# Attention probabilities transposed head by head (77 keys) instead of in 128-wide blocks, in a gated cross-attention and feed-forward kernel

## The chip, the cores and the metric

One NeuronCore of one Trainium2 chip runs the whole program. The time is device microseconds of one execution. The engines are named as in the profile: PE is TensorE's matmuls and PEld its weight loads, DVE is VectorE, ACT is ScalarE, POOL is GpSimd, SP is SyncE (here only a DMA queue).

## The reference, cut to what matters

Batch 16, 512 queries of width 512, 77 context tokens a batch, 16 heads of 32. All is float32.

```python
q = layernorm(x) @ Wq.T + bq              # (16, 512, 512)
k = ctx @ Wk.T + bk;  v = ctx @ Wv.T + bv # (16, 77, 512)
scores = einsum('bhnd,bhmd->bhnm', q, k) / sqrt(32)   # 16 heads, 512 x 77
attn = softmax(scores, axis=-1)
o = einsum('bhnm,bhmd->bhnd', attn, v)    # the values product
x = x + tanh(g_xattn) * (o @ Wo.T + bo)
x = x + tanh(g_ffn) * ffn(layernorm(x))   # 512 -> 2048 -> 512, with sines and relu
```

## The kernel before, in words

Three blocks follow each other: `setup` (weights turned and split, keys and values of all batches computed and kept in DRAM), `attention`, and `ffn`. The change touches the attention, and in the setup how the values are cleared, stored and loaded.

Projections, scores and output products run in three passes of split operands (`matmul3`, L56: high by high, high by low, low by high, type fp32r). The transposes of the probabilities and the values products take plain float32.

The attention handles a batch in four slots, one for each group `g` of four heads. A slot multiplies the queries of its four heads with a block-diagonal matrix of keys (`k_diag`, four times 77 = 308 columns) into two score banks, each of two tiles of 128 queries. DVE takes the peaks (L1063), ACT the exponentials with their sums (L1017), DVE the reciprocals (L1068), and POOL multiplies them into `probs` (L855). Two groups make a *pair* (eight heads, 616 columns of probabilities for each query); there are 32 pairs. `probs` has the 128 queries of a tile on the partitions and the 616 keys of a pair in a row, padded with zeros to 640.

The values product needs the keys on the partitions. So PE transposes `probs` (L900): the pair's 640 columns are five blocks `c` of 128 keys, and one block takes four transposes, one for each tile of queries, into one of two PSUM banks `t_bank`. The block is copied into `probsT` by DVE (`copy_probs`, L1059, blocks 0 to 2) or ACT (`copy_late_probs`, L1002, blocks 3 and 4), and the bank may be written again. In a transpose the data is what is loaded as weights, and the 128x128 identity is what is streamed; the profile writes this as 128*128 128x128 (weights, then streamed).

Blocks of 128 keys don't end where heads of 77 end. So a head's keys lie in one or two blocks, and `v_diag` holds its values at the same rows, with zeros elsewhere in the block (cleared once in setup, filled for each batch by twelve small DMAs, `load_values`). A head's product (L948) is one or two matmuls of 128 rows x 32 columns of weights with 512 queries streamed, added up in PSUM: six for each group of four heads, twelve a pair. The four heads of a group write four different strips of 32 partitions of one bank `m_bank`. In the profile each of these float32 matmuls is two instructions.

The order on PE is written out by hand, slot by slot (L966 to L988). In an even slot (`g` 0 or 2): scores, queries of the next slot, transposes of block 2 of the pair before, an output product of an earlier batch. In an odd slot (`g` 1 or 3): transposes of blocks 3 and 4, scores, queries of the next slot, output product, transposes of blocks 0 and 1 of the next pair, then the values products of the pair. Every engine runs its list in order and waits on counting semaphores: a transpose waits for the copy that last read its bank, a query projection for the subtraction that read its `m_bank` (`m_split`), the scores of a slot for their queries (`queries_lo`, L1078, on DVE).

The order on DVE in an even slot is peaks, `heads_lo` (L1085), peaks, copies of blocks 0 and 1, reciprocal, half of the rows of a layer norm or of a turn (L205, L214), copy of block 2, `queries_lo`, the other half of the rows, `gate_output` (L1091), reciprocal. In an odd slot it is peaks, peaks, `x_lo` (L1073) or the sums of a layer norm (L180), reciprocal, `queries_lo`, `gate_output`, reciprocal, `heads_lo`. ACT in an odd slot copies blocks 3 and 4, then exponentials, `queries_hi`, exponentials, `heads_hi` (L1029) twice.

Of the kernel before, what the change touches and what calls it, by code (L numbers as in the profile page):

```python
# [30 lines left out]
F32 = mybir.dt.float32  # L31
# [51 lines left out]
def gated_attention_ffn_kernel(nc, x, ctx_in, g_xattn, g_ffn, wq, bq, wk, bk, wv, bv, wo, bo,  # L83
# [13 lines left out]
    PC = -(-2 * GC // P)  # L97
    NC = -(-GC // P)
    FROM = (0, GC - (NC - 1) * P)
# [12 lines left out]
    assert N == 512 and D == 512 and G == KT == NT == 4 and B % CB == 0 and NC == 3 and PC == 5 and FT == 16  # L112
# [12 lines left out]
    with ExitStack() as whole:  # L125
# [130 lines left out]
        v_diag = [sb(att, f"v_diag{i}", [P, 2, NC, HG, 2 * DH]) for i in range(2)]  # L256
# [10 lines left out]
        pieces = [[], []]  # L267
        for second in range(2):
            for j in range(HG):
                r = FROM[second] + j * M  # L270
                end = r + M
                while r < end:
                    n = min(end, (r // P + 1) * P) - r
                    pieces[second].append((j, r // P, r % P, M - (end - r), n))
                    r += n
        assert len(pieces[0]) == len(pieces[1])
        PIECES = len(pieces[0])

        strips = []
        for j in range(HG):  # L280
            strip = []
            for second in range(2):
                of_head = [c for h, c, _, _, _ in pieces[second] if h == j]
                strip += [(second, c, i == 0, i == len(of_head) - 1) for i, c in enumerate(of_head)]
            strips.append(strip)
        assert all(len(strip) == len(strips[0]) for strip in strips)
        ends = [max((step, j) for j in range(HG) for step, piece in enumerate(strips[j]) if piece[0] == second)
                for second in range(2)]

# [8 lines left out]
        def load_values(queue, b, loaded):  # L298

            for second in range(2):  # L300
# [5 lines left out]
        def by_head(row):  # L306

            return row.rearrange("p (g h d) -> p g h d", g=G // 2, d=DH)

        def by_place(row):  # L310

            return row.rearrange("p (h g d) -> p g h d", g=G // 2, d=DH)

        def setup():
            with ExitStack() as st:  # L315
# [116 lines left out]
                def _(pool):  # L432
# [6 lines left out]
                    pool.memset(k_diag[:, :, :, :].bitcast(F32), 0.0)  # L439
# [4 lines left out]
                    pool.wait_ge(cleared, 2)  # L444
# [154 lines left out]
                def _(dve):  # L599
# [20 lines left out]
                    def values_sum(r, j):  # L620
                        n = v_rows(j)
                        dve.wait_ge(v_full, RT * r + j + 1)
                        if not (isinstance(r, int) and r == 0):
                            dve.wait_ge(v_stored[j], 16 * r)
                        dve.tensor_tensor(by_place(v_sum[j][0:n, :]), by_head(v_bank[j % 2][0:n, :]), by_head(bv_rows[0:n, :]),
                                          ALU.add)\
                           .then_inc(v_summed, 1)
# [86 lines left out]
        def attention(st):  # L714
# [4 lines left out]
            probs = [sb(st, f"probs{i}", [P, NT, PC * P]) for i in range(G // 2)]  # L719
            probsT = sb(st, "probsT", [P, PC, N])  # L720
# [22 lines left out]
            EARLY_C, LATE_C = range(NC), range(NC, PC)  # L743
# [34 lines left out]
            def transposed(pair, c):  # L778
                n = PC * pair + c + 1
                return n, (n - 1) % 2  # L780
# [71 lines left out]
            def _(pool):  # L852
# [14 lines left out]
                for i in range(G // 2):  # L867
                    pool.memset(probs[i][:, :, 2 * GC:PC * P], 0.0)
# [20 lines left out]
            def _(pe):  # L889
                def transpose_probs(pair, c):  # L890
                    n, bank = transposed(pair, c)
                    if c in (0, NC - 1):

                        pe.wait_ge(probs_ready, 4 * pair + (4 if c else 2))
                    if c >= 2:
                        pe.wait_ge(t_copied, NC * pair + c - 1)
                    elif pair:
                        pe.wait_ge(late_copied, 2 * (pair - 1) + c + 1)
                    for tile in range(NT):
                        tr = pe.transpose(t_bank[bank][:, tile * P:(tile + 1) * P],  # L900
                                          probs[pair % 2][:, tile, c * P:(c + 1) * P], ident[:, :])
# [29 lines left out]
                def value_products(pair, values):  # L931


                    pe.wait_ge(late_copied, 2 * (pair + 1))
                    b = pair // 2
                    if b == 0:
                        pe.wait_ge(first_values_loaded, 16 * PIECES * 2)
                    else:
                        pe.wait_ge(values_loaded[b % 2], 16 * PIECES * 2 * ((b + 1) // 2))
                    pe.wait_ge(m_split, values[0][0] - 2)  # L940
# [569 lines left out]
```

## Time and profile before

| | |
|---|---|
| median of 3 runs | 2146.89 us (2144.68 to 2148.01) |
| the profiled execution | 2147.3 us, its span 2145.5 us |
| PE busy | 2114.2 us (99%), 10321 matmuls |
| PEld busy | 1710.1 us (80%) |
| DVE busy | 1433.8 us (67%) |
| ACT busy | 1164.1 us (54%) |
| POOL busy | 398.6 us (19%) |
| granted TensorE clock, mean | 0.997 |

The span is the time from the first to the last instruction; the execution's own time lies 1.8 us above it. A line of a timeline gives the start of a run of like instructions, the time until the last of them ended, and their count. Matmuls overlap, so the mean duration of one is longer than the distance to the next. A row of one line's or one tile's instructions gives the least, median and largest duration of one in ns. A row of waits says who was waited for: total us, how often, the longest.

### The profile page before, as it was taken

The page shows a single profiled execution, that of the slowest core. Times are in us where ns is not written, and L with a number is a line of the kernel's source. Part 1 is how long each engine was busy: PE and PEld are TensorE (multiplying, and loading weights), DVE is VectorE, ACT ScalarE, POOL GpSimd, SP SyncE. Part 2 cuts the span into 40 slices and gives each one's busy share as a digit, 9 for nine tenths or more (in the row PEclk, how much of TensorE's full clock was granted, in tenths as well). Part 3 has the DMA queues.
Part 4 walks back from the last instruction along what each step waited for, and adds up shares of the span by engine and source line. Part 5 has one row for each costly group of instructions (what it writes and reads, how often), then busy time and mean ns, then how long its engine had stood idle before and what let it go on. Part 6 is the DMA issues. An engine that isn't in the chain of part 4 may idle for free.

```text
span 2145.5 us, 29054 instructions
## 1 busy us (share of the span) xinstructions
PE 2114.2 (99%) x10321; PEld 1710.1 (80%) x10321; DVE 1433.8 (67%) x2457; ACT 1164.1 (54%) x3463; POOL 398.6 (19%) x324
## 2 busy tenths in 40 slices
PE   8889999999999999999999999999999999999999
PEld 7767777777777678888888888888888888888887
DVE  4587877787777477666665666656666566566654
ACT  3387877777777455444445444444454444444443
POOL 3044444433443310010110101101101011010110
PEclk9999999999999999999999999999999999999999
DMA  7464445455544352231212312213123121231210
GB/s 217 128 144 110 121 126 120 121 119 117 128 113 101 118 146 75 59 77 50 51 59 59 79 59 41 77 41 79 59 59 79 53 46 62 57 79 59 40 40 20
DMA packets 372475, 181.88 MB, mean 85 GB/s; under 512 B 294374, under 2 KB 308938, under 8 KB 372330
## 3 DMA queue, kind: packets, MB, share of 16 engines
q1 hardware_dynamic: 371258, 179.52, 33.0%
q8 instruction: 81, 1.33, 0.3%
q0 software_dynamic: 640, 0.47, 0.1%
q14 instruction: 64, 0.52, 0.1%
q10 hardware_dynamic: 432, 0.04, 0.0%
HBM read 106.34 MB, written 56.85 MB: 76 GB/s over the span
## 4 chain that ended last, share of the span: by engine, by line
PE 63%; DVE 1%; ACT 0%; issue 0%; ACTq 0%; DVEq 0%
PE pair_bank L56 32%; PE m_bank L56 32%; DVE w_split L1402 0%; DVE hidden L1436 0%; DVE turns L1432 0%; DVE sine L1429 0%; ACT relu L1362 0%; ACT hidden L1371 0%; ACT turns L1373 0%; DVE stats L180 0%; DVE relu L1419 0%; DVE x_in L205 0%; ACT sine L1378 0%; DVE residual L1444 0%; DVE mean L190 0%
## 5 line engine op out<-in xcount | busy, mean ns | idle before, releaser
L56 PE MATMUL pair_bank<-w_split,relu 128*128 128x512 f32 x3072 | 738.4, 389 | 3.9 <-DVE relu L1419 3.2
L56 PE MATMUL m_bank<-xT,w_split 128*128 128x512 f32 x3024 | 726.4, 389 | 0.0
L56 PEld LDWEIGHTS pair_bank<-w_split,relu 128*128 128x128 f32 x3072 | 576.2, 188 | 125.4 <-issue 3.7
L56 PEld LDWEIGHTS m_bank<-xT,w_split 128*128 128x128 f32 x3024 | 567.5, 188 | 117.9
L1378 ACT ACTIVATE sine<-turns 128x512 f32<-128x512 f32 x256 | 161.8, 632 | 393.3 <-DVE turns L1432 393.3
L1017 ACT ACTIVATE exps<-pair_bank,lowest 128x77 f32<-128x77 f32 x1024 | 317.6, 352 | 59.8 <-DVE lowest L1063 59.7
L1362 ACT ACTIVATE relu<-hidden 128x512 fp32r<-128x512 f32 x256 | 161.9, 632 | 330.9 <-PE m_bank L56 231.6
L1419 DVE SCALAR_TENSOR_TENSOR relu<-hidden,relu 128x512 fp32r<-128x512 f32 x256 | 181.3, 708 | 201.7 <-ACT relu L1362 201.7
L1436 DVE SCALAR_TENSOR_TENSOR hidden<-sine,sine_gain,hidden 128x512 f32<-128x512 f32 x256 | 197.2, 770 | 169.9 <-ACT sine L1378 169.9
L200 POOL TENSOR_TENSOR rstd<-var_eps,minus_half 128x4 f32<-128x4 f32 x32 | 38.3, 1196 | 1198.3 <-DVE var_eps L196 1198.3
L1017 ACT ACTIVATION_READ_ACCUMULATOR exps<-pair_bank,lowest 128x1 f32 x1024 | 238.9, 234 | 0.0
L855 POOL TENSOR_TENSOR probs<-exps,exp_inv 128x616 f32<-128x616 f32 x128 | 158.6, 1239 | 300.1 <-DVE exp_inv L1068 300.1
L1432 DVE TENSOR_TENSOR turns<-turns,sine 128x512 f32<-128x512 f32 x256 | 192.2, 751 | 8.8
L56 PE MATMUL m_bank<-xT,wqT 128*128 128x512 f32 x768 | 188.1, 394 | 0.0
L1429 DVE TENSOR_SCALAR sine<-turns 128x512 f32<-128x512 f32 x256 | 122.2, 477 | 93.1 <-ACT turns L1373 92.6
L56 PE MATMUL m_bank<-woT,oT 128*128 128x512 f32 x720 | 180.0, 399 | 0.6 <-DVE oT L1085 0.6
L1373 ACT ACTIVATE turns<-m_bank,turns_phase 128x512 f32<-128x512 f32 x256 | 173.9, 679 | 0.0
L1371 ACT ACTIVATE hidden<-m_bank,columns 128x512 f32<-128x512 f32 x256 | 171.9, 671 | 1.9 <-PE m_bank L56 1.9
L56 PEld LDWEIGHTS m_bank<-xT,wqT 128*128 128x128 f32 x768 | 142.9, 190 | 27.1 <-DVE xT L1073 0.2
L56 PEld LDWEIGHTS m_bank<-woT,oT 128*128 128x128 f32 x720 | 133.4, 189 | 30.3 <-DVE oT L1085 1.5
L56 PEld LDWEIGHTS pair_bank<-k_diag,qT 128*128 128x128 f32 x768 | 111.2, 191 | 37.9 <-issue 30.9
L56 PE MATMUL pair_bank<-k_diag,qT 128*128 128x308 f32 x768 | 127.8, 315 | 9.9 <-PEq L315 5.3
(127 smaller groups left out, 1723.5 us busy)
## 6 DMA issues: line engine op xcount, KB each, us to landing
residual<-in_x_dram SPq DMA_DIRECT2D x64, 256.0 KB, 2.7
x_scratch<-residual SPq DMA_DIRECT2D x64, 256.0 KB, 2.1
x_in<-x_scratch SPq DMA_DIRECT2D x16, 1024.0 KB, 5.5
residual<-x_scratch SPq DMA_DIRECT2D x64, 256.0 KB, 3.3
out_dram<-residual SPq DMA_DIRECT2D x64, 256.0 KB, 2.1
quad_scratch<-x_in SPq DMA_DIRECT2D x60, 256.0 KB, 5.1
x_in<-quad_scratch SPq DMA_DIRECT2D x60, 256.0 KB, 4.4
x_in<-in_x_dram SPq DMA_DIRECT2D x8, 1024.0 KB, 5.6
```

Of the source, the lines that this page charges most:

```text
L56: mm = pe.matmul(out, stationary(s), moving(m), start=first and n == 0, stop=last and n == len(PASSES) - 1)
L200: pool.tensor_tensor(rstd[:, :], var_eps[:, :], minus_half[:, :], ALU.pow).then_inc(rstd_ready, 1)
L855: pool.tensor_tensor(probs[g // 2][:, HALF * half:HALF * (half + 1), g % 2 * GC:(g % 2 + 1) * GC] .rearrange("p n (h m) -> p n h m", m=M), ...
L1017: e = act.activation(exps[half][:, n, h * M:(h + 1) * M], pair_bank[half][:, n, h * M:(h + 1) * M], ACT.Exp, bias=lowest[half][:, i:i + 1] ...
L1362: act.activation(relu[f % 2][0][:, :], hidden[f % 2][:, :], ACT.Relu).then_inc(relu_hi, 1)
L1371: act.activation(hidden[f % 2][:, :], m_bank[f % 2][:, :], ACT.Identity, bias=b1_col[:, f % FT:f % FT + 1])
L1373: act.activation(turns[:, :], m_bank[f % 2][:, :], ACT.Identity, scale=0.1 / TWO_PI, bias=turns_phase[:, f % FT:f % FT + 1]).then_inc(h_re ...
L1378: act.activation(sine[:, :], turns[:, :], ACT.Sin, scale=TWO_PI_BELOW).then_inc(sine_ready, 1)
L1419: dve.scalar_tensor_tensor(out=relu[f % 2][1][:, :], in0=hidden[f % 2][:, :], scalar=0.0, in1=relu[f % 2][0][:, :].bitcast(F32), op0=ALU.m ...
L1429: dve.tensor_scalar(sine[:, :], turns[:, :], ROUND_MAGIC, ROUND_MAGIC, ALU.add, ALU.subtract)\
L1432: dve.tensor_tensor(turns[:, :], turns[:, :], sine[:, :], ALU.subtract).then_inc(part_ready, 1)
L1436: dve.scalar_tensor_tensor(out=hidden[f % 2][:, :], in0=sine[:, :], scalar=sine_gain[:, f % FT:f % FT + 1], in1=hidden[f % 2][:, :], op0=A ...
```

## The change: one block for each head

The blocks of the transposes are the heads: eight of 77 keys a pair, in place of five of 128. A transpose has 77 columns of weights and the same 128 columns of identity streamed; it writes 77 partitions. A head's values product is one matmul of 77 rows, eight a pair in place of twelve. The values of a batch lie as they are, 77 rows of 512, in `v_rows_of`, loaded by one DMA; nothing is cleared. The padding of `probs` is gone.

The transposes of heads 2 and 3 take the place of those of block 2, heads 4 and 5 that of blocks 3 and 4, heads 0 and 1 that of blocks 0 and 1. Heads 6 and 7 are transposed in the odd slot, after the queries and ahead of the output product. DVE copies heads 0 to 3 in the even slot and head 7 in the odd slot behind `queries_lo`; ACT copies heads 4 and 5 at the start of the odd slot and head 6 behind `queries_hi`, ahead of the second exponentials. The two groups' products follow each other, group by group.

```diff
-        v_diag = [sb(att, f"v_diag{i}", [P, 2, NC, HG, 2 * DH]) for i in range(2)]
+        v_rows_of = [sb(att, f"v_rows_of{i}", [P, D]) for i in range(2)]
...
         def load_values(queue, b, loaded):
-            for second in range(2):
-                for j, c, p0, m0, n in pieces[second]:
-                    h = HG * second + j
-                    queue.dma_start(v_diag[b % 2][p0:p0 + n, second, c, j, :],
-                                    v_rows_all[bass.ds(M * b + m0, n), 2 * DH * h:2 * DH * (h + 1)]).then_inc(loaded, 16)
+            queue.dma_start(v_rows_of[b % 2][0:M, :], v_rows_all[bass.ds(M * b, M)]).then_inc(loaded, 16)
...
-                    for i in range(2):
-                        pool.memset(v_diag[i][:, :, :, :, :], 0.0).then_inc(cleared, 1)
...
-            probs = [sb(st, f"probs{i}", [P, NT, PC * P]) for i in range(G // 2)]
-            probsT = sb(st, "probsT", [P, PC, N])
+            probs = [sb(st, f"probs{i}", [P, NT, 2 * GC]) for i in range(G // 2)]
+            probsT = sb(st, "probsT", [P, 2 * HG, N])
...
+            DVE_HEADS, ACT_HEADS = (0, 1, 2, 3, 7), (4, 5, 6)
+            def copies_until(pair, h):
+                of_dve = h in DVE_HEADS
+                heads = DVE_HEADS if of_dve else ACT_HEADS
+                return (t_copied if of_dve else late_copied), len(heads) * pair + heads.index(h) + 1
...
-                def transpose_probs(pair, c):
-                    n, bank = transposed(pair, c)
-                    if c in (0, NC - 1):
-                        pe.wait_ge(probs_ready, 4 * pair + (4 if c else 2))
-                    if c >= 2:
-                        pe.wait_ge(t_copied, NC * pair + c - 1)
+                def transpose_probs(pair, h):
+                    n, bank = transposed(pair, h)
+                    if h in (0, HG):
+                        pe.wait_ge(probs_ready, 4 * pair + (4 if h else 2))
+                    if h >= 2:
+                        pe.wait_ge(*copies_until(pair, h - 2))
                     elif pair:
-                        pe.wait_ge(late_copied, 2 * (pair - 1) + c + 1)
+                        pe.wait_ge(*copies_until(pair - 1, h + 2 * HG - 2))
                     for tile in range(NT):
-                        tr = pe.transpose(t_bank[bank][:, tile * P:(tile + 1) * P],
-                                          probs[pair % 2][:, tile, c * P:(c + 1) * P], ident[:, :])
+                        tr = pe.transpose(t_bank[bank][0:M, tile * P:(tile + 1) * P],
+                                          probs[pair % 2][:, tile, h * M:(h + 1) * M], ident[:, :])
...
                 def value_products(pair, values):
-                    pe.wait_ge(late_copied, 2 * (pair + 1))
+                    pe.wait_ge(*copies_until(pair, DVE_HEADS[-1]))
+                    pe.wait_ge(*copies_until(pair, ACT_HEADS[-1]))
...
-                    for step in range(len(strips[0])):
-                        if step == 1:
-                            pe.wait_ge(m_split, values[1][0] - 2)
+                    for second, (n, bank, _) in enumerate(values):
+                        pe.wait_ge(m_split, n - 2)
                         for j in range(HG):
-                            second, c, first, last = strips[j][step]
-                            mm = pe.matmul(m_bank[values[second][1]][j * DH:(j + 1) * DH, :],
-                                           v_diag[b % 2][:, second, c, j, pair % 2 * DH:(pair % 2 + 1) * DH],
-                                           probsT[:, second * (NC - 1) + c, :], start=first, stop=last)
-                            if (step, j) in (ends[0], ends[1]):
-                                mm.then_inc(m_full, 1)
+                            column = (2 * (pair % 2) + second) * P + j * DH
+                            mm = pe.matmul(m_bank[bank][j * DH:(j + 1) * DH, :], v_rows_of[b % 2][0:M, column:column + DH],
+                                           probsT[0:M, second * HG + j, :], start=True, stop=True)
+                        mm.then_inc(m_full, 1)
...
                         if s.queries:
                             queries(b + (g == 3), (g + 1) % G, *s.queries[:2])
-                        if not s.odd and s.pair is not None:
-                            transpose_probs(s.pair, NC - 1)
+                        if s.pair is not None:
+                            for h in (6, 7) if s.odd else (2, 3):
+                                transpose_probs(s.pair, h)
                         if s.output:
                             block_output(*s.output)
...
                     if s.queries:
                         queries_hi((g + 1) % G, *s.queries[:2])
+                    if s.odd and s.pair is not None:
+                        copy_late_probs(s.pair, 6)
                     if s.score:
                         exponentials(2 * G * b + 2 * g + 2, 1)
...
                     if s.queries:
                         queries_lo((g + 1) % G, *s.queries[1:])
+                    if s.odd and s.pair is not None:
+                        copy_probs(s.pair, 7)
```

## Rows read from the trace of the kernel before

**Rows 1.** The page's slices: the granted TensorE clock in tenths.
```profile
PEclk9999999999999999999999999999999999999999
```

**Rows 2.** Windows: stretch, us; busy PE, PEld, DVE, ACT, POOL (count); clock, DMA.
```profile
200.00:700.00 500.00, 500.00 (x2958) 387.90 (x2956) 389.80 (x715) 373.39 (x1845) 202.00 (x165) 1.00 0.49 117
131.00:150.50 19.50, 16.84 (x107) 12.40 (x106) 18.13 (x36) 17.51 (x90) 10.43 (x9) 1.00 0.49 72
```

**Rows 3.** Waits from 200 to 700 us: total us, times, longest.
```profile
ACT oT L1029 <- PE m_bank L948: 66.5, 50, 2.4
...
DVE oT L1085 <- ACT oT L1029: 63.1, 25, 2.5
...
PEld pair_bank L56 <- DVE qT L1078: 0.5, 2, 0.2
```

**Rows 4.** Timeline of PE: start, us, instructions, in one pair.
```profile
307.01 1.03 PE L900 MATMUL t_bank<-ident,probs 128*128 128x128 f32 x8
307.97 2.78 PE L948 MATMUL m_bank<-probsT,v_diag 128*32 128x512 f32 x24
310.68 1.96 PE L56 MATMUL pair_bank<-k_diag,qT 128*128 128x308 f32 x12
...
315.25 0.60 PE L900 MATMUL t_bank<-ident,probs 128*128 128x128 f32 x4
315.61 3.04 PE L56 MATMUL m_bank<-woT,oT 128*128 128x512 f32 x12
```

**Rows 5.** Values products and transposes, 300 to 400 us: least, median, largest ns.
```profile
L948 PEld LDWEIGHTS m_bank<-probsT,v_diag x120: 106/110/110, 308.0 to 388.0; 128*32 128x32 f32 x120
L948 PE MATMUL m_bank<-probsT,v_diag x120: 592/592/617, 308.0 to 388.4; 128*32 128x512 f32 x120
...
L900 PEld LDWEIGHTS t_bank<-ident,probs x100: 138/140/142, 306.8 to 397.4; 128*128 128x128 f32 x100
L900 PE MATMUL t_bank<-ident,probs x100: 270/272/273, 307.0 to 397.5; 128*128 128x128 f32 x100
```

**Rows 6.** Timeline of PEld: loads of the third and the sixth round of these products.
```profile
308.43 0.13 PEld L948 LDWEIGHTS m_bank<-probsT,v_diag 128*32 128x32 f32 x4 [0.30 <-issue]
...
309.71 0.13 PEld L948 LDWEIGHTS m_bank<-probsT,v_diag 128*32 128x32 f32 x4 [0.30 <-issue]
```

**Rows 7.** Setup's context transposes, 36.46 to 36.50 us: 52 rows, then 128.
```profile
L476 PE MATMUL pair_bank<-ident,ctx_raw x2: 263/296/329, 36.3 to 36.4; 52*128 52x52 f32 x1, 128*128 128x128 f32 x1
```

**Rows 8.** Groups by line and shape: the block copies, and one operation on 52 partitions.
```profile
L1059 DVE COPY probsT<-t_bank 128x512 f32<-128x512 f32 x75 | 48.6, 676 | 0.4 <-PE t_bank L900 0.4
...
L1002 ACT ACTIVATE probsT<-t_bank 128x512 f32<-128x512 f32 x52 | 28.8, 621 | 6.8 <-PE t_bank L900 6.8
...
L625 DVE TENSOR_TENSOR v_sum<-pair_bank,bv_rows 128x512 f32<-128x512 f32 x8 | 5.5, 690 | 10.1 <-PE pair_bank L56 10.1
...
L625 DVE TENSOR_TENSOR v_sum<-pair_bank,bv_rows 52x512 f32<-52x512 f32 x4 | 2.7, 680 | 6.3 <-PE pair_bank L56 6.3
```

**Rows 9.** Timelines of DVE and PE where an even slot meets an odd one.
```profile
297.85 0.68 DVE L1059 COPY probsT<-t_bank 128x512 f32<-128x512 f32 x1
298.45 0.73 DVE L1078 SCALAR_TENSOR_TENSOR qT<-m_bank,columns,qT 128x512 fp32r<-128x512 f32 x1
...
300.02 0.74 DVE L1091 SCALAR_TENSOR_TENSOR residual<-m_bank,tanh_g,residual 128x512 f32<-128x512 f32 x1
...
300.84 0.80 DVE L1063 TENSOR_REDUCE lowest<-pair_bank 128x8 f32<-128x616 f32 x1
...
298.92 1.03 PE L900 MATMUL t_bank<-ident,probs 128*128 128x128 f32 x8
299.71 1.94 PE L56 MATMUL pair_bank<-k_diag,qT 128*128 128x308 f32 x12
```

**Rows 10.** Waits from 120 to 152 us, the first pairs.
```profile
PE t_bank L900 <- DVE probsT L1059: 2.0, 2, 1.6
```

**Rows 11.** The values' DMA issues on SP's queue in the attention: least, median, largest ns.
```profile
L303 SPq DMA_DIRECT2D v_diag<-v_scratch x180: 269/307/720, 121.5 to 667.7; - x180
```

More of the change, by code:

```diff
@@ L111, in gated_attention_ffn_kernel @@
     NVEC = 4 * FT + 2 * G
-    assert N == 512 and D == 512 and G == KT == NT == 4 and B % CB == 0 and NC == 3 and PC == 5 and FT == 16
+    assert N == 512 and D == 512 and G == KT == NT == 4 and B % CB == 0 and FT == 16
     x1 = nc.dram_tensor("x1_scratch", [B, N, D], F32).ap()
@@ L264, in gated_attention_ffn_kernel @@
         first_values_loaded = sem(whole, "first_values_loaded")
-        pieces = [[], []]
-        for second in range(2):
[L269 to L288, printed above, removed]
         def load_keys(queue, b, pair, loaded):
@@ L776, in attention, with transposed @@
             values_of = {s.pair: s.values for s in slots if s.values}
-            def transposed(pair, c):
-                n = PC * pair + c + 1
+            def transposed(pair, h):
+                n = 2 * HG * pair + h + 1
                 return n, (n - 1) % 2
@@ L968, in _ @@
                     if not s.score:
+                        for h in (4, 5) if s.odd else (2, 3):
+                            transpose_probs(s.pair, h)
                         block_output(*s.output)
-                        for c in LATE_C if s.odd else (NC - 1,):
-                            transpose_probs(s.pair, c)
+                        for h in (6, 7) if s.odd else ():
+                            transpose_probs(s.pair, h)
                     else:
                         if s.odd and s.pair is not None:
-                            for c in LATE_C:
-                                transpose_probs(s.pair, c)
+                            for h in (4, 5):
+                                transpose_probs(s.pair, h)
                         for half in range(2):
@@ L979, in _ @@
                             queries(b + (g == 3), (g + 1) % G, *s.queries[:2])
[L980 to L981 removed]
+                        if s.pair is not None:
+                            for h in (6, 7) if s.odd else (2, 3):
+                                transpose_probs(s.pair, h)
                         if s.output:
@@ L984, in _ @@
                         if s.next_pair is not None:
-                            for c in range(NC - 1):
-                                transpose_probs(s.next_pair, c)
+                            for h in (0, 1):
+                                transpose_probs(s.next_pair, h)
                     if s.values:
@@ L997, in _, with copy_late_probs @@
             def _(act):
-                def copy_late_probs(pair):
-                    for c in LATE_C:
-                        n, bank = transposed(pair, c)
-                        act.wait_ge(t_full, n)
-                        act.activation(probsT[:, c, :], t_bank[bank][:, :], ACT.Copy).then_inc(late_copied, 1)
+                def copy_late_probs(pair, h):
+                    n, bank = transposed(pair, h)
+                    act.wait_ge(t_full, n)
+                    act.activation(probsT[0:M, h, :], t_bank[bank][0:M, :], ACT.Copy).then_inc(late_copied, 1)
                 def x_hi(b):
@@ L1034, in _ @@
                     if s.odd and s.pair is not None:
-                        copy_late_probs(s.pair)
+                        for h in (4, 5):
+                            copy_late_probs(s.pair, h)
                     if s.score:
@@ L1053, in _, with copy_probs @@
             def _(dve):
-                def copy_probs(pair, c):
-                    n, bank = transposed(pair, c)
+                def copy_probs(pair, h):
+                    n, bank = transposed(pair, h)
                     dve.wait_ge(t_full, n)
-                    if c == 0 and pair:
+                    if h == 0 and pair:
                         dve.wait_ge(m_full, values_of[pair - 1][0][0])
-                    dve.tensor_copy(probsT[:, c, :], t_bank[bank][:, :]).then_inc(t_copied, 1)
+                    dve.tensor_copy(probsT[0:M, h, :], t_bank[bank][0:M, :]).then_inc(t_copied, 1)
                 def peaks(unit, half):
@@ L1104, in _ @@
                         if s.pair is not None:
-                            for c in range(NC - 1):
-                                copy_probs(s.pair, c)
+                            for h in (0, 1):
+                                copy_probs(s.pair, h)
                         if s.score:
@@ L1113, in _ @@
                         if s.pair is not None:
-                            copy_probs(s.pair, NC - 1)
+                            for h in (2, 3):
+                                copy_probs(s.pair, h)
                     else:
```

25 lines of the change are left out of this document (5 added, 20 removed).

## The prediction

> **What bounds the kernel now.** I read the granted clock first: full speed in every slice, so no time is lost to it [rows 1]. Then the busy times by stretch. From 200 to 700 us, 25 of the 32 pairs, PE is busy for all 500 us, DVE for 390 and ACT for 373 [rows 2]. As a busy PE may hide gaps, I then read the waits of that stretch: the scores waited twice for DVE's query subtraction, 0.5 us in all, while ACT and DVE each stood idle about 2.5 us a pair until the values products were done (66.5 us in 50 waits, of which the first of each pair is the long one; 63.1 us in 25) [rows 3]. So the steady attention is bound by the sum of PE's work, and what the change adds to or takes from that sum is the first term. Last I read PE's timeline for the distances between its instructions, since durations overlap [rows 4].
>
> **A transpose.** Eight of them take 1.03 us to the end of the last [rows 4], and one lasts 0.272 us [rows 5]: (1.03 - 0.272) / 7 = 108 ns from one to the next. The four at 315.25 give (0.60 - 0.272) / 3 = 109 ns, and the output product behind them starts on time, at 315.61. I take 0.1085 us.
>
> **A values product.** The 24 instructions of a pair start in rounds of four, one for each head. The weight loads of the third and the sixth round stand 309.71 - 308.43 = 1.28 us apart, three rounds [rows 6]: 0.427 us a round. Six rounds are 2.56 us; from the first product to the scores behind them pass 2.71 us [rows 4], so entering and leaving costs 0.15 us, which stays.
>
> **What sets the price of a transpose with 77 columns.** This decides the sign, and no such transpose is in the trace. A product of 512 streamed columns lasts 592 ns, a transpose of 128 lasts 272 [rows 5]: 320 ns for 384 columns, 0.833 ns a column. That gives 512 columns 427 ns, which is the distance between rounds, and 128 columns 107 ns, which is the distance between transposes. So both are bound by what they stream. The change leaves that as it is: 128 columns of identity for each transpose. What shrinks from 128 to 77 columns is the weight load. Is it what binds? In setup a transpose of 52 rows, then one of 128, follow a change of shape, so that their loads are uncovered: 263 and 329 ns [rows 7]. By the rate, a transpose of 52 streamed columns should last 272 - 76 x 0.833 = 209 ns; it is 54 longer, and the one of 128 is 329 - 272 = 57 longer. So a load of 128 columns costs some 55 ns when nothing hides it, half of the 107 that a transpose streams, and it is hidden in a run of them. I take 0.1085 us for the new transpose too. The lower end is a price that goes with the columns loaded, 0.1085 x 77/128 = 0.065 us. Between lies the slope of the two loads, 110 ns for 32 columns and 140 for 128 [rows 5], 0.31 ns a column: 51 columns fewer save 16 ns, 0.092 us. The upper end is a load that stays uncovered, as after the changes of shape in setup: 0.1085 + 0.055 = 0.164 us. Nothing points there, as all transposes of a run have one shape. I take the row nearest in what it does, today's transpose.
>
> The Trainium skill (TensorE: Matmul & The Clock Gate, section "LDWEIGHTS (loading the stationary operand)") gives a load as its columns divided by 1.2, in ns. As an estimate from that page, 128 columns take 107 ns and 77 take 64, which would fit the distance of 108 just as well with the load as its bound. The uncovered loads of some 55 ns [rows 7] speak against it for transposes; what it would make of the time is rival A.
>
> **PE's sum.** Twelve transposes more: 12 x 0.1085 = 1.30 us. Two rounds fewer, as eight products in place of twelve are four rounds of four heads in place of six: 2 x 0.427 = 0.85 us. Net +0.45 us a pair, and for 32 pairs +14.3 us. There is one more run of transposes a pair; entering and leaving a run costs no more than some ns (315.25 + 4 x 0.1085 = 315.68, and the output product's first matmul was already in at 315.61), so nothing.
>
> **The copies.** They cost by their row, not by partitions: 680 ns on 52 and 690 on 128 [rows 8]. So DVE gets two more copies, 2 x 0.676 = 1.35 us a pair, and ACT one more, 0.62 us. Both have 2.5 us of idle time ahead of the values products [rows 3], which covers copy 7 and copy 6, both in the odd slot. What waits behind them: on ACT the second exponentials, then POOL's probabilities of that half, which PE wants only a slot later; on DVE the gate of the output, which the second group's products wait for. PE itself gets two runs more between its queries and those products, 8 x 0.1085 = 0.87 us, so the gate comes no later against PE than before. The new waits, heads 6 and 7's copies ahead of the next pair's transposes and of the values products, have the output product (12 matmuls, some 2.8 us) between the transposes and the wait. Cost: nothing; without the cover up to 0.68 us a pair.
>
> The tight place is the even slot. There copy 3 is added ahead of `queries_lo`, which the next slot's scores wait for. In the pair at 298 us copy 2 starts at 297.85 and `queries_lo` ends at 298.45 + 0.73 = 299.18; the scores start at 299.71 [rows 9]. One copy later it ends at 299.86; the scores, behind four more transposes (0.44 us), are due at 300.15. It fits by 0.3 us, so I cost it at nothing. The peaks at 300.84 come behind a gate at 300.02 [rows 9]; both are up to 0.7 us later on DVE against 0.44 on PE, and the odd slot's idle time takes the rest up.
>
> **The first pairs.** From 131 to 150.5 us DVE is busy 18.13 of 19.5 us [rows 2], and transposes waited 2.0 us for its copies [rows 10]. There the two copies count instead of PE's net: 1.35 - 0.45 = 0.9 us more for a pair, for one pair or two. I take +1 us, the ends are 0 and 2.
>
> **Loads and clearing.** Twelve issues of some 0.307 us a batch on SP's queue become one [rows 11]. SP gets to its stores about 3.4 us sooner, but nobody on PE waited for a load in the steady stretch. POOL's clearing in setup is long done when the first values come. Nothing either way.
>
> **Sum.** 14.3 + 1 = 15.3 us on the profiled execution's own 2147.3: 2162.6. The median of the runs lies 0.4 us below that execution, so 2162 us, 0.7% slower.
>
> **Rivals.**
>
> *A. A transpose costs by the columns loaded.* For it: 108 ns would also fit a load as the bound. Against it: the rate of 0.833 ns that explains both forms, and the uncovered loads. Fully proportional: 32 x 0.065 - 20 x 0.1085 = -0.09, with the products -0.94 us a pair, -30 us: 2117. At 0.092 us it is 32 x 0.092 - 2.17 - 0.85 = -0.08 us a pair: 2144. It ends on the other side, faster, for any transpose under (2.17 + 0.85) / 32 = 94 ns.
>
> *B. DVE becomes late in the even slot.* For it: only 0.3 us of room at 299.86 against 300.15, and rows there that last longer than elsewhere. Then copy 3 delays `queries_lo` and with it the scores. If its whole 0.68 us lands on PE in the sixteen slots with a layer norm, +11 us: 2173; in all 32, +22: 2184. Against it: the scores waited for DVE twice in 25 pairs.
>
> *C. The heads' products of 77 rows don't run four at a time.* Then 16 instructions take 16 x 0.427 = 6.8 us, 4.3 more than now, +137 us: about 2300. Against it: the heads still write four different strips, and only the count of rows is new. With it goes the upper end above: 0.164 us would make 32 x (32 x 0.164 - 2.17 - 0.85) = +71 us, 2219.
>
> **How the numbers follow.** Forecast 0.73, A 0.13, B 0.12, C 0.02. The forecast's own range is 2158 to 2167. The range for 8 in 10 reaches up into B as far as 2177 and down to 2154, where a transpose costs 0.100 us; it leaves out most of A, the far end of B, and C. A measurement of this kernel tells some 0.2%, 4.3 us, from no change. Of A's 0.13, 0.10 is faster and 0.03 within 0.2%; with 0.01 for gaps that take up the forecast's cost, same is 0.04; slower is the rest, 0.86.
>
> **What would show it.** Right: transposes of 77 columns 108 ns apart, runs of eight in 1.03 us; four rounds of products, some 1.85 us from the first product to the scores; pairs 0.45 us longer; no waits of PE on DVE or ACT between 200 and 700 us. Wrong: runs of eight in 0.8 us or less (A), scores waiting for `queries_lo` (B), rounds of fewer than four (C), or a clock below full speed in a slice.

## The result and the profile after

The changed kernel takes 2169.08 us (median of 4 runs, 2168.72 to 2171.05) against 2147.28 us (2144.68 to 2148.01) for the kernel before beside it: ratio 1.0106, 95% interval 1.0088 to 1.0123, so 21.8 us slower. The forecast was 2162, the range 2154 to 2177. The direction and the main term held; two terms that I had costed at almost nothing make up the difference. The time lies above the forecast's own range of 2158 to 2167; the part of the range that it fell in was added for rival B, which, as shown below, isn't the cause. The profiled run took 2168.72 us, its span is 2166.9. Of all runs below, one execution of 5524 us with the late layer norm is left out of the times.

Cut at the first values product of the third pair, of the last but one and of the last, the two spans give the table below. The forecast in it is split by its own terms: ahead of the first cut lie three pairs' transposes and two pairs' products, 3 x 1.30 - 2 x 0.85, and the +1 for the first pairs; behind the last one pair's products.

| stretch | before, us | after, us | difference | forecast |
|---|---|---|---|---|
| to the third pair | 170.87 | 177.83 | +6.96 | +3.2 |
| 28 pairs | 546.09 | 557.50 | +11.41 | +12.6 |
| the last pair | 11.26 | 14.88 | +3.62 | +0.45 |
| behind it (rest, FFN) | 1417.26 | 1416.70 | -0.56 | -0.85 |

PE's timeline after, in the steady attention, answers to [rows 4]:

```profile
317.05 1.04 PE L862 MATMUL t_bank<-ident,probs 128*77 128x128 f32 x8
318.01 1.92 PE L905 MATMUL m_bank<-probsT,v_rows_of 77*32 77x512 f32 x16
319.87 1.96 PE L56 MATMUL pair_bank<-k_diag,qT 128*128 128x308 f32 x12
...
328.04 1.03 PE L862 MATMUL t_bank<-ident,probs 128*77 128x128 f32 x8
328.83 1.94 PE L56 MATMUL pair_bank<-k_diag,qT 128*128 128x308 f32 x12
...
337.98 1.92 PE L905 MATMUL m_bank<-probsT,v_rows_of 77*32 77x512 f32 x16
```

Eight transposes of 77 columns take 1.03 to 1.04 us, as eight of 128 did. From the first values product to the scores pass 1.86 us in place of 2.71. From one pair's products to the next pass 19.97 us; before it was 19.57. The durations, from 300 to 400 us, answer to [rows 5] (least, median, largest ns):

```profile
L862 PEld LDWEIGHTS t_bank<-ident,probs x160: 143/147/148, 303.9 to 397.6; 128*77 128x77 f32 x160
L862 PE MATMUL t_bank<-ident,probs x160: 270/272/334, 304.1 to 397.7; 128*77 128x128 f32 x160
L905 PE MATMUL m_bank<-probsT,v_rows_of x80: 592/592/617, 318.0 to 399.3; 77*32 77x512 f32 x80
```

A load of 77 columns lasts 147 ns; one of 128 lasted 140. The busy times and waits from 200 to 700 us, and the copies' group, answer to [rows 2, 3, 8]:

```profile
200.00:700.00 500.00, 499.96 (x3001) 404.26 (x2999) 403.88 (x756) 375.90 (x1823) 204.62 (x162) 1.00 0.47 116
```

```profile
ACT oT L986 <- PE m_bank L905: 55.7, 50, 2.0
...
DVE oT L1045 <- ACT oT L986: 43.3, 26, 1.7
...
PEld pair_bank L56 <- DVE qT L1038: 0.5, 2, 0.2
```

```profile
L1019 DVE COPY probsT<-t_bank 77x512 f32<-77x512 f32 x125 | 80.2, 672 | 0.0
```

PE is as busy as before and waits for DVE 0.5 us in all. DVE's idle time until the values products are done went from 2.5 to 1.7 us a pair: copies lie in it now.

**The first pairs.** PE's timeline after; in brackets, idle time before the run and whose end released it:

```profile
132.66 1.04 PE L862 MATMUL t_bank<-ident,probs 128*77 128x128 f32 x8
135.44 0.63 PE L862 MATMUL t_bank<-ident,probs 128*77 128x128 f32 x4 [1.74 <-ACT probsT L959]
136.27 0.99 PE L862 MATMUL t_bank<-ident,probs 128*77 128x128 f32 x4 [0.20 <-DVE probsT L1019]
137.19 3.64 PE L905 MATMUL m_bank<-probsT,v_rows_of 77*32 77x512 f32 x16
140.76 3.09 PE L56 MATMUL pair_bank<-k_diag,qT 128*128 128x308 f32 x12
...
156.42 0.63 PE L862 MATMUL t_bank<-ident,probs 128*77 128x128 f32 x4 [0.82 <-ACT probsT L959]
157.28 0.66 PE L862 MATMUL t_bank<-ident,probs 128*77 128x128 f32 x4 [0.22 <-DVE probsT L1019]
```

At 132.66 stand heads 6 and 7, at 135.44 and 136.27 heads 0 and 1 of the next pair. Nothing lies between them: the first two pairs' odd slots have no output product yet. So each wait for a copy is paid. Behind the first one the granted clock falls to its lower level, 1.2 GHz, for most of two windows, and 16 products last 3.64 us in place of 1.92. It falls there in all five profiles with this order of the first pairs. Windows (busy PE, PEld, DVE, ACT, POOL; clock; DMA), where the kernel before had 1.00:

```profile
135.00:140.00 5.00, 4.36 (x24) 1.63 (x24) 2.29 (x11) 3.32 (x18) 3.11 (x3) 0.65 0.66 98
140.00:145.00 5.00, 5.00 (x22) 4.02 (x19) 2.80 (x5) 2.06 (x11) 2.18 (x3) 0.67 0.56 90
```

**The end of the attention.** Where no scores are left, the changed order puts heads 2 and 3 ahead of the output product, right behind the values products (timeline and a window):

```profile
739.29 1.26 PE L862 MATMUL t_bank<-ident,probs 128*77 128x128 f32 x8 [2.04 <-DVE probsT L1019]
740.30 4.58 PE L56 MATMUL m_bank<-woT,oT 128*128 128x512 f32 x12
```

```profile
740.00:745.00 5.00, 5.00 (x19) 4.02 (x20) 1.35 (x3) 0.00 (x0) 1.28 (x1) 0.66 0.00 0
```

PE waits 2.04 us, and the output product runs at the lower clock, 4.58 us where 3.05 is usual.

### The profile page after: what moved, and what is told of

Same layout as the page of the kernel before. It is cut to its first block, busy times and chain, and to the rows that moved or that the text cites. A ratio compares the mean times of both kernels' runs of the same rounds, so it can differ in the third digit from the quotient of the medians.

```text
span 2166.9 us, 29258 instructions
## 1 busy us (share of the span) xinstructions
PE 2131.7 (98%) x10449; PEld 1744.6 (81%) x10449; DVE 1460.3 (67%) x2521; ACT 1179.6 (54%) x3495; POOL 397.1 (18%) x309
## 4 chain that ended last, share of the span: by engine, by line
PE 63%; DVE 1%; ACT 0%; issue 0%; ACTq 0%; DVEq 0%
PE pair_bank L56 31%; PE m_bank L56 31%; DVE w_split L1365 0%; DVE hidden L1399 0%; DVE turns L1395 0%; DVE sine L1392 0%; ACT relu L1325 0%; ACT hidden L1334 0%; ACT turns L1336 0%; DVE stats L177 0%; DVE relu L1382 0%; DVE x_in L202 0%; ACT sine L1341 0%; DVE residual L1407 0%; DVE mean L187 0%
## 5 line engine op out<-in xcount | busy, mean ns | idle before, releaser
L974 ACT ACTIVATION_READ_ACCUMULATOR exps<-pair_bank,lowest 128x1 f32 x1024 | 225.0, 220 | 0.0
L862 PEld LDWEIGHTS t_bank<-ident,probs 128*77 128x77 f32 x1024 | 120.7, 147 | 25.3 <-DVE probsT L1019 4.0
```

The lines of the kernel that those rows point to most:

```text
L862: tr = pe.transpose(t_bank[bank][0:M, tile * P:(tile + 1) * P], probs[pair % 2][:, tile, h * M:(h + 1) * M], ident[:, :])
L974: e = act.activation(exps[half][:, n, h * M:(h + 1) * M], pair_bank[half][:, n, h * M:(h + 1) * M], ACT.Exp, bias=lowest[half][:, i:i + 1] ...
```

## The experiments

The theory: PE's sum sets the steady pairs, with a transpose bound by its 128 streamed columns; the rest of the loss is two places where the order leaves a copy uncovered. Rivals: the loaded columns or some other part of a transpose set its price; DVE's copies delay the even slot.

**The two terms of the sum, one by one.** On the kernel before: the transposes of blocks 0 to 2 made twice, 12 more a pair; and, in another kernel, eight products in place of twelve, which leaves out the second pieces of the heads that straddle two blocks.

```diff
-                    for tile in range(NT):
+                    for tile in (*range(NT), *(range(NT) if c < NC else ())):
```
```diff
-                    for step in range(len(strips[0])):
+                    for second in range(2):
...
+                            c = [piece[1] for piece in strips[j] if piece[0] == second][0]
...
```

> The kernel before (2147.3 us) with the transposes of blocks 0, 1 and 2 issued twice in place, into the same bank, with nothing else changed: the twelve more transposes a pair of the change, alone, without more copies or waits. Theory 1 (PE's sum of work sets the steady time, a transpose costs what it streams): 32 x 12 x 0.1085 = +41.7 us, 2189, pairs 1.30 us longer. Rival (the cost of the change came from the copies and the waits for them): much less than that, under +20 us, as no copy is added.

> The kernel before with eight values products a pair in place of twelve, of 128 rows as before: the second piece of each head that lies in two blocks is left out (so that part of the values sum is left out). It is the two rounds fewer of the change, alone. Theory 1: 32 x 2 x 0.427 = -27.3 us, 2120, pairs 0.85 us shorter. Rival (another engine sets the pair as soon as PE gets shorter, DVE with 15.6 of 19.6 us first): less than 20 us off.

Measured: 2186.43 us (ratio 1.0181, 1.0164 to 1.0198), pairs of 20.88 us, +1.315: 109.6 ns a transpose. PE's timeline shows 16 in one run:

```profile
335.03 2.96 PE L56 MATMUL m_bank<-woT,oT 128*128 128x512 f32 x12
337.83 1.91 PE L900 MATMUL t_bank<-ident,probs 128*128 128x128 f32 x16
```

The other: 2120.12 us (0.9871, 0.9855 to 0.9888), pairs of 18.68, -0.885, here from one pair's products to the next pair's:

```profile
301.38 1.92 PE L946 MATMUL m_bank<-probsT,v_diag 128*32 128x512 f32 x16
...
320.05 1.92 PE L946 MATMUL m_bank<-probsT,v_diag 128*32 128x512 f32 x16
```

Their sum is +1.315 - 0.885 = +0.43 us a pair, against +0.41 measured for the whole change; of the two times it is +39.3 - 27.0 = +12.3 us. The steady part of the loss is these two terms.

**The load.** On the kernel after, seven of the eight transposes load 128 columns again (51 that nobody reads).

```diff
...
+                        wide = M if h == HG - 1 else P
...
-                                          probs[pair % 2][:, tile, h * M:(h + 1) * M], ident[:, :])
+                                          probs[pair % 2][:, tile, h * M:h * M + wide], ident[:, :])
...
```

> The changed kernel with the loads of seven of eight heads' transposes widened from 77 back to 128 columns (the rows beyond 77 that come out are not used). Stream theory (a transpose is bound by the 128 columns of identity that it streams, its load is hidden): transposes stay 108 to 109 ns apart, time 2169 within 1 us, 2170 with the clearing of the padding. Load theory (the columns loaded count, even if other costs hid the gain): transposes of 128 columns are dearer than those of 77 by up to 43 ns, 28 x 32 of them up to 38 us, 2170 to 2207.

Measured: 2169.0 us (ratio 1.0095, 1.0078 to 1.0112), as the kernel after. Its timeline of PE:

```profile
325.07 1.03 PE L865 MATMUL t_bank<-ident,probs 128*128 128x128 f32 x8
325.86 2.98 PE L56 MATMUL m_bank<-woT,oT 128*128 128x512 f32 x12
```

It is the same 1.03 us for eight. In these runs of transposes the loaded columns have no price, in either direction: rival A is refuted.

**The first pairs.** On the kernel after, where a slot has no output product, heads 6 and 7 are transposed ahead of the queries, copy 6 goes ahead of ACT's first exponentials and copy 7 behind DVE's peaks.

```diff
+                        early = s.odd and s.pair is not None and s.output is None
+                        if early:
+                            for h in (6, 7):
+                                transpose_probs(s.pair, h)
                         if s.queries:
                             queries(b + (g == 3), (g + 1) % G, *s.queries[:2])
-                        if s.pair is not None:
+                        if s.pair is not None and not early:
...
```

> The changed kernel with one edit: in the two early odd slots that have no output product (batch 0 group 3, batch 1 group 1), heads 6 and 7 are transposed ahead of the queries, ACT copies head 6 ahead of the first exponentials, and DVE copies head 7 behind the peaks. Theory 1: the waits of 1.7 and 0.2 us of the next transposes for these copies go in both slots, the clock does not fall to half at 135 us, and the first products and scores take 1.9 us and 2.0 us in place of 3.6 and 3.1: 4 to 5 us less, 2164 to 2165. Theory 2: no change. Rival of theory 1: the chain from scores over exponentials to probabilities sets the pace there anyway, so the wait moves and only 1 us or less is gained, 2168.

Measured: 2163.15 us (2162.51 to 2164.04; ratio 1.0071, 1.0054 to 1.0087), 5.9 us below the kernel after by the medians. PE's timeline and a window of it:

```profile
128.81 1.04 PE L862 MATMUL t_bank<-ident,probs 128*77 128x128 f32 x8
129.60 2.99 PE L56 MATMUL m_bank<-xT,wqT 128*128 128x512 f32 x12
132.44 1.03 PE L862 MATMUL t_bank<-ident,probs 128*77 128x128 f32 x8
133.40 1.07 PE L905 MATMUL m_bank<-probsT,v_rows_of 77*32 77x512 f32 x8
```

```profile
135.00:140.00 5.00, 4.23 (x27) 3.13 (x28) 4.68 (x14) 4.02 (x23) 3.92 (x4) 1.00 0.64 92
```

The queries now cover the copies, the first values product comes at 133.40 in place of 137.19, and the clock stays at 2.4 GHz. The third pair's products start at 172.03: 5.8 of the 6.96 us are back, and what is left, 1.16 us, is less than the 3.2 of the forecast. How much of the 5.8 was wait and how much clock isn't separated by this edit.

**The end.** On the kernel after, the output product ahead of heads 2 and 3 where no scores are left; run in two jobs, the second beside the kernel after on the same chip.

```diff
-                        for h in (4, 5) if s.odd else (2, 3):
+                        for h in (4, 5) if s.odd else ():
                             transpose_probs(s.pair, h)
                         block_output(*s.output)
-                        for h in (6, 7) if s.odd else ():
+                        for h in (6, 7) if s.odd else (2, 3):
```

> The changed kernel (2169.1 us) with one edit: in the two slots behind the last scores, the output product comes ahead of the transposes of heads 2 and 3 again, as in the kernel before. Theory 1 (the cost over the sum of PE's work lies at the two ends of the attention, as waits of PE for copies, followed by a stretch at half the TensorE clock): PE's gap of 2.0 us ahead of those transposes goes, the clock stays full there, the last pair's 14.9 us shrinks by 2 to 3 us, time 2166 to 2167. Theory 2 (the cost is the sum of work alone, spread over all pairs): no change, 2169 within 1 us.

> The kernel after, once more, as the base of the two others of its family on this chip: 2168 to 2171 us.

> The tail edit alone, once more, beside the kernel after on the same chip. If the 2.4 us that the last pair lost in its trace are the end of the path: 2 to 2.5 us below the kernel after of this job (2166 to 2167). If the FFN stage takes them back, as a clock or an input that comes no earlier would: within 0.7 us of it.

Measured: 2168.96 us (ratio 1.0096, 1.0079 to 1.0112) in the first job, a miss, as the kernel after. In the second 2167.41 (2166.66 to 2168.86; 1.0086, 1.0073 to 1.0099), beside 2170.29 for the kernel after (2166.37 to 2171.14; 1.0101, 1.0086 to 1.0115). In the trace the stretch did what was expected:

```profile
740.64 3.06 PE L56 MATMUL m_bank<-woT,oT 128*128 128x512 f32 x12 [0.58 <-DVE oT L1045]
743.54 1.03 PE L862 MATMUL t_bank<-ident,probs 128*77 128x128 f32 x8
745.01 1.17 PE L862 MATMUL t_bank<-ident,probs 128*77 128x128 f32 x8 [0.43 <-DVE probsT L1019]
```

The last pair takes 12.49 us in both profiles, and not 14.88. But the second profile of the kernel after shows 13.32, with the same wait of 2.04 us and no fall of the clock behind it:

```profile
738.51 1.26 PE L862 MATMUL t_bank<-ident,probs 128*77 128x128 f32 x8 [2.04 <-DVE probsT L1019]
739.52 3.03 PE L56 MATMUL m_bank<-woT,oT 128*128 128x512 f32 x12
```

So in these profiles the order costs 0.8 us, and the clock some 1.5 more where it falls. It fell in three of the four profiles with that order: the early edit and the wide load end the same way, with 14.75 and 14.85 us. The intervals of the times overlap; the second job has the expected sign, the first shows none, and the size isn't settled by them. The traces show what hid the gain in the first job's profile: its first scores start at 102.81 us, against 101.73 in that of the kernel after, and its 28 pairs take 558.6 us against 557.5. Of the first, 1.0 us is one run of 48 products in setup that takes 9.45 us in place of 8.46; why is open. The first scores spread from 101.6 to 104.7 over all profiles.

**Both, and DVE's layer norm.** The two edits together, and then with all four tiles of an even slot's layer norm, or of its turn, behind the query subtraction (before, two of them lie ahead of copies 2 and 3).

```diff
-                        if g == 0 and 1 <= b and b + 2 <= B:
-                            normalise(dve, b + 3, x_rows[b % 2], range(HALF))
...
-                            normalise(dve, b + 3, x_rows[b % 2], range(HALF, NT))
+                            normalise(dve, b + 3, x_rows[b % 2], range(NT))
```

> Both edits (the tail's order, and the early slots' copies). Theory 1: they are independent and add up, 6 to 8 us less than the changed kernel, 2161 to 2163; what is left over the kernel before is 32 pairs of 0.41 to 0.45 us, 13 to 14 us. Theory 2: 2169.

> Both schedule edits (early odd slots and the tail), and VectorE does the layer-norm work of an even slot in one piece behind the query copy and not half of it ahead of copies 2 and 3. Theory: what scattered the kernel with both edits over 2160.4 to 2166.0 us are pairs in which the layer-norm pair of VectorE takes 2.9 us in place of 1.9 and PE then loses 0.3 to 0.6 us on copies 2, 3 and the query copy. With that work behind them no pair loses, and the time is 2160 us or a little less, within 1 us from run to run. Rival (the layer-norm work is off the path, or moves the loss to the odd slot that follows, where copies 4 and 5 come behind it): 2163 to 2166 us, and a wait of PE on VectorE in the odd slots.

Measured: 2164.48 us with both (2160.36 to 2165.99; ratio 1.0073, 1.0056 to 1.009), a miss: no better than the early edit alone. Its timelines of DVE, of PE and of POOL show where rival B bites:

```profile
260.24 2.91 DVE L202 TENSOR_SCALAR x_in<-x_in,mean,rstd 128x512 f32<-128x512 f32 x2
263.07 1.27 DVE L1026 COPY probsT<-t_bank 77x512 f32<-77x512 f32 x2
264.27 0.73 DVE L1045 SCALAR_TENSOR_TENSOR qT<-m_bank,columns,qT 128x512 fp32r<-128x512 f32 x1
```

```profile
263.90 1.17 PE L862 MATMUL t_bank<-ident,probs 128*77 128x128 f32 x8
265.06 1.95 PE L56 MATMUL pair_bank<-k_diag,qT 128*128 128x308 f32 x12
```

```profile
260.24 1.28 POOL L829 TENSOR_TENSOR residual<-residual,bo_rows 128x512 f32<-128x512 f32 x1 [4.18 <-DMA residual<-in_x_dram]
261.47 1.40 POOL L820 TENSOR_TENSOR probs<-exps,exp_inv 128x616 f32<-128x616 f32 x1
```

Two tiles of layer norm take 2.91 us, copies 2 and 3 and the subtraction come late, and the scores start 1.16 us behind the transposes in place of 0.79. Six of the 28 pairs are longer so; in the kernel after two are, by 0.33 and 0.56 us, and in the kernel before two are as well, by 0.36 and 0.46. What lengthens the two tiles is in the trace: each starts when an instruction of POOL is running or starts too, and ends some 0.28 us after that has ended. So do all 22 such tiles of that kernel from 200 to 700 us (279 to 289 ns after it, 0.63 to 1.57 us long); the 24 tiles with no POOL instruction beside them took 0.53 to 0.54 us. POOL's `residual` starts when its DMA has landed, which differs from pair to pair. With the layer norm behind the copies no pair is longer, and the 28 pairs take 556.6 us in place of 559.2; the rows of that group (half of the first 24 tiles lie ahead of the copies, half behind), with both edits and then with the late layer norm, from 200 to 700 us:

```profile
L202 DVE TENSOR_SCALAR x_in<-x_in,mean,rstd 128x512 f32<-128x512 f32 x24 | 21.2, 923 | 0.0
```

```profile
L202 DVE TENSOR_SCALAR x_in<-x_in,mean,rstd 128x512 f32<-128x512 f32 x24 | 13.5, 623 | 0.0
```

The time is 2163.08 us (2161.97 to 2163.98; ratio 1.0064, 1.0051 to 1.0077), not the 2160 expected. The pairs gained 2.6 us; of that, 1.5 went between the first scores and the first values product (33.6 us in place of 32.05), and the profile's first scores came 1.4 us later. What is left over the kernel before beside it, 14.9 us, is about the 15.3 that the forecast added, with the new waits at nothing.

**Row halves.** What else can a transpose's stream be cut by? Each one in two halves of 64 rows, lower into bank 0 and upper into bank 1: first on the kernel with both edits, then on the kernel before, with loads of 128 columns, last with block 2 left whole.

```diff
+                        for half in range(2):
+                            rows = slice(half * R, (half + 1) * R)
+                            tr = pe.transpose(t_bank[half][:, i * R:(i + 1) * R],
+                                              probs[pair % 2][rows, tile, block_c * P:(block_c + 1) * P], ident[rows, rows])
...
```

> Both edits of e3_both, and each transpose cut in two halves of 64 queries (64 rows, 64 streamed columns of identity), the lower halves of two heads into one bank, the upper ones into the other; the copies move the same amount. Stream theory, if two halves run side by side on their rows: eight transposes become 16 halves, 8 x 0.055 = 0.44 us, and entering and leaving a run costs some 0.1 us each (in setup a transpose of 52 rows followed one of 128 after 0.2 us in place of 0.11): 0.64 in place of 0.87 us a run, -0.9 us a pair, -29 us against e3_both's 2164: 2135, below the kernel before. If halves don't run side by side: 16 x 0.055 + 0.2 = 1.08 us a run, +27 us: 2191. If a transpose costs a fixed 0.108 us whatever it streams: 16 x 0.108 = 1.73 us a run, +110 us: 2275.

> The kernel before, with each of its five 128x128 transposes of a pair and tile cut into two halves of 64 rows that run side by side, the lower into bank 0 and the upper into bank 1, in three runs a pair in place of five; the loads stay 128 columns wide. What sets the 66 to 69 ns between pairs of halves that were seen with 77 columns? If two loads of 77 columns, one behind the other: with 128 columns a pair of halves comes every 107 to 110 ns, nothing is gained, three runs a pair each pay some 0.13 us of entering and leaving: 2155 to 2162 us. If it is the stream of 64 rows and a fixed part: 69 ns again, 20 x 0.040 = 0.8 us less a pair, 0.4 us of entering and leaving more, -0.4 x 32 = -13: 2134 us.

> As the kernel before with row halves, but block 2, the run of four transposes by itself, stays whole; the two runs of eight stay in halves. Theory (halves 0.061 us apart in place of 0.109, and each run of halves pays some 0.09 us more to enter and 0.12 more to leave): a run of eight gains 7 x 0.109 - (0.109 + 6 x 0.061) = 0.29 and pays about 0.22, a run of four gains 0.10 and pays 0.21, so leaving block 2 whole gives 0.11 us a pair back: pairs of 19.36 us in place of 19.475, 3.7 us less in 32 pairs, 6 us below the kernel before (ratio 0.997). Rival (what a run of halves pays is not by run, but by the turn from tile to tile, and halves are free): no better than with all three runs in halves, ratio 0.9986 or more.

Measured: 2162.74 us (ratio 1.007, 1.0053 to 1.0087), pairs of 19.86; then 2145.70 (2143.24 to 2147.42, beside 2148.19; 0.9986, 0.9978 to 0.9995), pairs of 19.48; last 2143.23 (2141.41 to 2144.42, beside 2150.38; 0.9965, 0.9953 to 0.9977), pairs of 19.33. PE's timeline of the second, then of the last:

```profile
303.28 2.96 PE L56 MATMUL m_bank<-woT,oT 128*128 128x512 f32 x12
306.17 0.71 PE L913 MATMUL t_bank<-ident,probs 64*128 64x64 f32 x16
306.81 2.78 PE L962 MATMUL m_bank<-probsT,v_diag 128*32 128x512 f32 x24
...
314.18 0.46 PE L913 MATMUL t_bank<-ident,probs 64*128 64x64 f32 x8
314.57 3.05 PE L56 MATMUL m_bank<-woT,oT 128*128 128x512 f32 x12
```

```profile
317.45 0.60 PE L907 MATMUL t_bank<-ident,probs 128*128 128x128 f32 x4
317.80 3.04 PE L56 MATMUL m_bank<-woT,oT 128*128 128x512 f32 x12
```

With a duration of 0.223 us, eight pairs of halves in 0.71 us and four in 0.46 give 0.25 / 4 = 62 ns from pair to pair; the first step is about 110. The two halves of a pair start within 4 ns of each other. Two loads of 128 columns lie in each step, also side by side, so a load takes up less than 62 ns there, and the load theory of that run fell. The expected 2135 and 2134 us fell as well: a run of halves starts 2.89 us behind the output product's start, where the run of 16 whole ones above does after 2.80, and the scores or the output product behind it start some 0.15 us after the last half against 0.03. So what a run pays there is about 0.2 us and not 0.13 (ahead of the values products it pays less: 0.15 against 0.20 behind it); a run of four halves, 0.39 us to the output product, is worse than four whole ones, 0.35, even without its later start. Leaving block 2 whole was worth 0.15 us a pair, and that kernel is faster than both.

## Why the prediction came out as it did

- **What bounds it** held: PE's sum sets the steady pairs; 0.5 us of waits in 500 us, as before.
- **The price of a transpose**, the step that decides the sign, held: 1.03 us for eight. The hidden load stood the test by the wide load. The rate of 0.833 ns a streamed column wasn't tested by it; the halves come near, with 62 ns for 64 streamed columns where the rate gives 53. As an estimate from the Trainium skill (TensorE: Matmul & The Clock Gate, section "LDWEIGHTS (loading the stationary operand)"), one load of 128 columns would take 107 ns; a pair of halves that needs two such loads came every 62 ns, so the measurement decides against the rule for these transposes.
- **A values product** held: four rounds, 1.86 us to the scores. Rival C didn't come.
- **PE's sum**: +0.45 us a pair was forecast, +0.41 measured.
- **"The new waits, heads 6 and 7's copies ..., have the output product ... between the transposes and the wait. Cost: nothing"** is the step that failed. It is true of all but the first two pairs and the last. The first two odd slots have no output product. Where no scores are left the order puts the product on the other side; there the dear wait, 2.04 us, is one that the prediction doesn't name, of heads 2 and 3 for the copies of heads 0 and 1. I read the order of a steady slot and applied it to all. The prediction's own price without cover, "up to 0.68 us a pair", was too low too: copy 6 stands behind the exponentials on ACT, so the wait was 1.74 us.
- **The first pairs**, "+1 us, the ends are 0 and 2", is the mis-sized term: I counted DVE's two copies and not the waits' order, and left out that a waiting PE can lose its clock. The stretch lost 6.96 us in place of 3.2, and the early edit got 5.8 back; the end lost 3.62 in place of 0.45. That the sum stayed inside the range is in part luck: the range reached up to 2177 for rival B, and the 28 pairs, where B would act, lost less than forecast, 11.4 in place of 12.6. The sign that was named for the clock, a slice below full speed, couldn't show its fall: a slice of the page is 54 us long and reads 9 throughout, before and after; windows of 5 us show it.
- **The even slot** held in nearly all pairs; rival B costs two pairs 0.33 and 0.56 us, and before the change two pairs lost 0.36 and 0.46.
- **Loads and clearing** left no mark: the first scores start at 101.73 us, before at 101.75.

## What to carry to other kernels

Price an instruction by what binds it (here the streamed columns), and find that by comparing two shapes of it in the trace before; a change that shrinks the other dimension then buys nothing. An argument of the form "this work covers that wait" has to be checked in the slots that lack the work: the first ones and the last ones. When PE waits near a place where it isn't fed, count the clock as a possible second price, since here it was of the size of the wait.

## What was new about the hardware

- After waits of 1.74 and 0.20 us, with only transposes between them, the granted clock was below full in two windows of 5 us (0.65 and 0.67); after one of 1.36 us in the next slot, and one of 1.88 us at 144.2 us with the early edit, it didn't fall. The same wait of 2.04 us was followed by 0.66 in one execution and by the full clock in another.
- Two transposes of 64 rows, in different row halves and banks, run side by side; a pair comes every 62 ns with 128 loaded columns. With 77 columns, 16 halves took 0.77 us in place of 0.71: fewer loaded columns were slower. Why is open.
- A TENSOR_SCALAR of DVE, the layer norm's on a 128x512 tile (L202, before L205), that starts while a TENSOR_TENSOR of POOL is running, or with it, ended 279 to 289 ns after it in all 22 cases with both edits, and 281 to 292 ns after it in all 20 of the kernel before; it lasted up to 1.6 us, against 0.49 to 0.54 with none beside it. That POOL holds it up is read from these times; no run took the POOL instruction away.
